# Left-over edge tiles of four edge passes: first record and gather at the start of the pass, message in three bf16 pieces, sums added bank by bank, last placing DMAs from two engines

## The reference

```python
x = _layernorm(x + gat(x))      # three attention layers
# edge layer ("edges"):
h = maximum(concat([x[row], edge_attr], 1) @ W1a + b1a, 0) @ W1b + b1b
ssum = segment_sum(h, col, N)   # then mean, an MLP, residual, norm
# relation layer ("relations"):
for r in range(8):
    out += segment_sum(where(edge_type == r, x[src] @ weight[r], 0), dst, N)
# two-layer signed GCN ("near", then "far"), for w+ and w-:
agg = segment_sum(h[src] * (dinv[src] * w * dinv[tgt])[:, None], tgt, N)
```

## Time and profile before

| | us |
|---|---|
| median of 3 runs | 4453.6 (4448.56 to 4459.53) |
| profiled execution, its span | 4502.7 |
| TensorE busy | 3132.8 (70%) |
| VectorE busy | 3224.2 (72%) |
| ScalarE busy | 1435.4 (32%) |
| GpSimd busy | 1405.7 (31%) |

### The profile page before, as it was taken

One profiled execution on the slowest core, in us unless ns is written; L12 is line 12 of the kernel. 1 busy time (PEld: TensorE's weight loads), 2 busy tenths in 40 slices (PEclk: granted clock), 3 DMA queues, 4 the chain that ended last, 5 costly groups with the idle time before them and its releaser, 6 DMA issues. The chain is left out here.

```text
span 4502.7 us, 84639 instructions
## 1 busy us (share of the span) xinstructions
PE 3132.8 (70%) x29061; PEld 2437.5 (54%) x29061; DVE 3224.2 (72%) x7791; ACT 1435.4 (32%) x2737; POOL 1405.7 (31%) x1198
## 2 busy tenths in 40 slices
PE   0087777777238348158499985588888769959995
PEld 0054444444102112112499984287888769959995
DVE  7766666665489699699577763377767579967886
ACT  0034444444025125035399981233333200000000
POOL 0055555555264454554000000266666300000000
PEclk9978888888569679579699996599999879979997
DMA  8845555545458358267377740111111024413331
GB/s 323 322 129 143 153 144 148 157 131 149 147 172 264 114 166 263 88 200 246 106 221 221 222 148 12 56 24 23 24 23 24 14 67 111 109 28 102 88 91 47
DMA packets 413507, 587.19 MB, mean 130 GB/s; under 512 B 76420, under 2 KB 301787, under 8 KB 412709
## 3 DMA queue, kind: packets, MB, share of 16 engines
q1 hardware_dynamic: 366005, 447.98, 34.2%
q0 software_dynamic: 37728, 66.91, 5.5%
q10 hardware_dynamic: 9360, 66.90, 3.7%
HBM read 340.05 MB, written 234.93 MB: 128 GB/s over the span
## 5 line engine op out<-in xcount | busy, mean ns | idle before, releaser
L846 POOL DMA_INDIRECT slots<-bc_rec,idx x496 | 484.6, 977 | 410.4 <-ACT bc_rec L807 294.4
L1284 POOL DMA_INDIRECT rp_rows<-rel_rows,slot_rel x390 | 412.1, 1057 | 431.7 <-POOLq L118 182.3
L1106 PE MATMUL psum<-a_probs,z 128*65 128x512 f32 (+1 forms) x1050 | 445.7, 557 | 145.0 <-DVE a_probs L1039 145.0
L1320 DVE TENSOR_SCALAR rp_hot_src<-rp_key_rows,lane 128x384 bf16<-128x384 f16 x1560 | 383.5, 317 | 202.0 <-issue 88.5
L1534 PE MATMUL psum<-rel_pieces,rp_hot_src 128*128 128x192 bf16 x4680 | 452.1, 249 | 94.3 <-issue 75.8
L1074 ACT ACTIVATE a_tops<-a_tops,a_s_low 128x1024 f32<-128x1024 f32 (+2 forms) x300 | 284.1, 947 | 569.6 <-DVE a_tops L1030 569.1
L1534 PEld LDWEIGHTS psum<-rel_pieces,rp_hot_src 128*128 128x128 bf16 x4680 | 390.4, 99 | 128.8 <-issue 107.0
L483 POOL DMA_INDIRECT slots<-h,idx x192 | 327.6, 1706 | 352.3 <-DMA h<-recs 304.1
L1106 PEld LDWEIGHTS psum<-a_probs,z 128*65 128x65 f32 x1050 | 121.8, 137 | 469.4 <-DVE a_probs L1039 301.5
L703 DVE TENSOR_SCALAR bc_first_t<-bc_ramp,bc_key_t 128x128 f16<-128x128 f16 x500 | 136.5, 273 | 307.8 <-PE psum L729 172.7
L1030 DVE SCALAR_TENSOR_TENSOR a_tops<-table,a_s_rest,big 128x1024 f32<-128x1024 f32 (+2 forms) x300 | 309.3, 1031 | 32.8 <-DMA big<-shift_rows 32.8
(11 more groups left out here) (438 smaller groups left out, 6855.1 us busy)
## 6 DMA issues: line engine op xcount, KB each, us to landing
a_counts<-edge_counts SPq DMA_DIRECT2D x150, 512.0 KB
slots<-big ACTq DMA_DIRECT2D x65, 1005.0 KB
ep_rec<-slots SPq DMA_DIRECT2D x65, 1005.0 KB, 6.2
edge_counts<-bc_counts SPq DMA_DIRECT2D x12, 3125.0 KB
hot_rows<-ep_hot_src SPq DMA_DIRECT2D x325, 96.0 KB, 4.5
sp_hot_src<-hot_rows SPq DMA_DIRECT2D x325, 96.0 KB, 2.0
sq_hot_src<-hot_rows SPq DMA_DIRECT2D x325, 96.0 KB, 2.0
a_counts<-edge_counts SPq DMA_DIRECT2D x75, 282.5 KB
```

The source lines that it names most:

```text
L846: pool.indirect_dma_start(k.slots, bass.IndirectOffsetOnAxis(k.idx[:, first + t:first + t + 1], 0), rec[:, j, t, :], None).then_inc(scatte ...
L1106: last = nc.tensor.matmul(sums[:, a:b], k.z[:, s, 0:D + 1], probs[:, a:b], start=s == 0, stop=True, skip_group_check=True)
L1284: pool.indirect_dma_start(rows[:, n % ROW_SLOTS, s, 0:width], None, table, bass.IndirectOffsetOnAxis(k.slot_rel[:, at:at + 1], 0))\
L1320: last = v.tensor_scalar(hot_src[:, n % HOT_SLOTS, rel, :], key_rows[:, n % 2, :], k.lane[:, rel:rel + 1], None, ALU.is_equal)
```

## The change

It touches `edge_pass`, and a little of the sorting before it.

- SP loads the first left-over tile's record as its first instruction of the pass. VectorE makes `left_no` from it before its first chunk, and POOL gathers `left_row` before its own first fetch. The loop then loads the record and gathers the rows of the tile that comes next. It does so after the last tile too, so the list gets a second tile of zero records (`zero_idx` has two columns, and one more scatter clears them).
- `left_message`: VectorE makes the one-hot matrix in bf16 instead of float32, then the message, and splits the message into three bf16 pieces with four more operations. None of it waits for the evacuation or the placing.
- TensorE does three bf16 matmuls for each of the 25 tiles (75, and in `ep` 75 more with 3 columns). It posts `left_sum` once for each bank of four tiles, and only bank 6 waits for the evacuation.
- VectorE waits for the placing DMAs behind the message and adds each bank when it is posted. Ahead of the last bank it waits for the record of the next tile and makes the next `left_no`. In `rp` the two halves of `acc` are added after the loop.
- SP issues that next record's load when all seven banks are posted. POOL, in its loop, gathers the next rows and waits until they have landed.
- The DMAs that place the last triple are issued by SP and ACT in turn, two each.

```diff
-                pool.indirect_dma_start(k.slots, bass.IndirectOffsetOnAxis(k.zero_idx[:, 0:1], 0),
+                for y in range(2):
+                    pool.indirect_dma_start(k.slots, bass.IndirectOffsetOnAxis(k.zero_idx[:, y:y + 1], 0),
...
-        left_row, left_out = sb("left_row", [P, width]), sb("left_out", [P, FIELD])
-        left_dst = k.big
+        left_row, left_out, left_rest = sb("left_row", [P, width]), sb("left_out", [P, FIELD]), sb("left_rest", [P, FIELD])
+        left_parts = sb("left_parts", [P, 3, FIELD], BF16)
+        left_dst = k.big[:, :, :].rearrange("p t c -> p (t c)").bitcast(BF16)[:, 0:NPAD].rearrange("p (t c) -> p t c", c=P)
+        left_cols = {"edges": FIELD, "relations": D}.get(kind, H)
+        LEFT_BANKS = (NT + 3) // 4
+        LEFT_STEPS = {"edges": 6, "relations": 5, "near": 6, "far": 5}[kind]
...
+        def last_parts():
+
+            j = NTRIPLE - 1
+            return [(k.acc[at:at + rows_now, tile, 0:wide], totals[m:m + rows_now, j % 2, b % SLOTS, :])
+                    for b in bins_of(j) for m, rows_now, tile, at in bin_parts(b)]
...
+                def place_last():
+                    sp.wait_ge(evacuated, NTRIPLE)
+                    for to, source in last_parts()[0::2]:
+                        sp.dma_start(to, source).then_inc(placed[(NTRIPLE - 1) % 2], 16)
...
+                sp.dma_start(left_rec[:, :], k.slots[LEFT:LEFT + P, :]).then_inc(left_in, 16)
...
-                for j in range(placed_to, NTRIPLE):
+                for j in range(placed_to, NTRIPLE - 1):
                     place(j)
+                place_last()
                 left_count = sp.value_load(k.left_tiles[0:1, 0:1], min_val=1, max_val=EPAD // P)
                 with sp.Fori(0, left_count) as i:
-                    sp.wait_ge(left_free, i + 1)
+                    sp.wait_ge(left_sum, i * LEFT_BANKS + LEFT_BANKS)
                     sp.sem_inc(fence, 1)
-                    sp.dma_start(left_rec[:, :], k.slots[bass.ds(i * P + LEFT, P), :]).then_inc(left_in, 16)
+                    sp.dma_start(left_rec[:, :], k.slots[bass.ds(i * P + LEFT + P, P), :]).then_inc(left_in, 16)
...
+                pool.wait_ge(left_idx, 1)
+                pool.indirect_dma_start(left_row[:, :], None, table,
+                                        bass.IndirectOffsetOnAxis(left_no[:, 0:1], 0)).then_inc(left_rows, 16)
...
-                    pool.wait_ge(left_idx, i + 1)
+                    pool.wait_ge(left_idx, i + 2)
                     pool.sem_inc(fence, 1)
                     pool.indirect_dma_start(left_row[:, :], None, table,
                                             bass.IndirectOffsetOnAxis(left_no[:, 0:1], 0)).then_inc(left_rows, 16)
+                    pool.wait_ge(left_rows, i * 16 + 32)
+                    pool.sem_inc(fence, 1)
...
+                def left_message(i):
+                    taken = 0
+
+                    def link(ins):
+                        nonlocal taken
+                        taken += 1
+                        ins.then_inc(left_step, 1)
+                        dve.wait_ge(left_step, i * LEFT_STEPS + taken)
+                        dve.sem_inc(fence, 1)
+
+                    out = left_out[:, 0:left_cols]
+                    v.tensor_scalar(left_dst, k.all_rows[:, :, :], left_rec[:, H + 4:H + 5], None, ALU.is_equal)\
+                        .then_inc(left_hot, 1)
+                    dve.wait_ge(left_rows, i * 16 + 16)
+                    dve.sem_inc(fence, 1)
...
+                    rest = left_rest[:, 0:left_cols]
+                    link(v.tensor_copy(left_parts[:, 0, 0:left_cols], out))
+                    link(v.tensor_tensor(rest, out, left_parts[:, 0, 0:left_cols], ALU.subtract))
+                    link(v.tensor_copy(left_parts[:, 1, 0:left_cols], rest))
+                    v.tensor_tensor(left_parts[:, 2, 0:left_cols], rest, left_parts[:, 1, 0:left_cols], ALU.subtract)\
+                        .then_inc(left_msg, 1)
...
+                dve.wait_ge(left_in, 16)
+                left_number()
...
-                dve.sem_inc(left_free, 1)
-                dve.wait_ge(evacuated, NTRIPLE)
-                for y in range(2):
-                    dve.wait_ge(placed[y], parts_placed(y, NTRIPLE))
-                if relations:
-                    chain.link(v.tensor_tensor(k.acc[:, :, 0:D], k.acc[:, :, 0:D], k.acc[:, :, D:2 * D], ALU.add))
                 left_count = dve.value_load(k.left_tiles[0:1, 0:1], min_val=1, max_val=EPAD // P)
                 with dve.Fori(0, left_count) as i:
-                    dve.wait_ge(left_in, i * 16 + 16)
+                    left_message(i)
+                    for y in range(2):
+                        dve.wait_ge(placed[y], parts_placed(y, NTRIPLE))
                     dve.sem_inc(fence, 1)
...
-                    dve.sem_inc(left_msg, 1)
-                    dve.wait_ge(left_sum, i + 1)
-                    dve.sem_inc(fence, 1)
-                    to, main = k.acc, D if relations else H
-                    for b in range(0, NT, 4):
-                        n = min(4, NT - b)
-                        bank = k.psum[:, b // 4, :].rearrange("p (t c) -> p t c", c=P)
-                        last = v.tensor_tensor(to[:, b:b + n, 0:main], to[:, b:b + n, 0:main], bank[:, 0:n, 0:main], ALU.add)
+                    for b in range(LEFT_BANKS):
+                        if b == LEFT_BANKS - 1:
+                            dve.wait_ge(left_in, i * 16 + 32)
+                            dve.sem_inc(fence, 1)
+                            left_number()
+                        dve.wait_ge(left_sum, i * LEFT_BANKS + b + 1)
+                        dve.sem_inc(fence, 1)
+                        first, n = 4 * b, min(4, NT - 4 * b)
+                        main = min(left_cols, H)
+                        bank = k.psum[:, b, :].rearrange("p (t c) -> p t c", c=P)
+                        to = k.acc[:, first:first + n, 0:main]
+                        last = v.tensor_tensor(to, to, bank[:, 0:n, 0:main], ALU.add)
                     if edges:
                         last = v.tensor_tensor(k.acc[:, :, H:FIELD], k.acc[:, :, H:FIELD],
                                                k.psum[:, 7, 0:NT * 3].rearrange("p (t c) -> p t c", c=3), ALU.add)
-                    last.then_inc(left_free, 1)
-                dve.wait_ge(left_free, 2)
+                    last.then_inc(left_step, 1)
+                    dve.wait_ge(left_step, i * LEFT_STEPS + LEFT_STEPS)
+                    dve.sem_inc(fence, 1)
+                if relations:
+                    chain.link(v.tensor_tensor(k.acc[:, :, 0:D], k.acc[:, :, 0:D], k.acc[:, :, D:2 * D], ALU.add))
...
+                act.wait_ge(evacuated, NTRIPLE)
+                for to, source in last_parts()[1::2]:
+                    act.dma_start(to, source).then_inc(placed[(NTRIPLE - 1) % 2], 16)
...
-                pe.wait_ge(evacuated, NTRIPLE)
...
-                    main = D if relations else H
-                    got = left_row if relations else left_out
+                    main = min(left_cols, H)
                     for t in range(NT):
-                        last = nc.tensor.matmul(k.psum[:, t // 4, t % 4 * P:t % 4 * P + main], left_dst[:, t, :],
-                                                left_out[:, 0:main], start=t % 4 == 0, stop=True, skip_group_check=True)
+                        if t // 4 == 6 and t % 4 == 0:
+                            pe.wait_ge(evacuated, NTRIPLE)
+                        for piece in range(3):
+                            last = nc.tensor.matmul(k.psum[:, t // 4, t % 4 * P:t % 4 * P + main], left_dst[:, t, :],
+                                                    left_parts[:, piece, 0:main], start=t % 4 == 0 and piece == 0, stop=True,
+                                                    skip_group_check=True)
+                        if t % 4 == 3:
+                            last.then_inc(left_sum, 1)
                     if edges:
                         for t in range(NT):
-                            last = nc.tensor.matmul(k.psum[:, 7, t * 3:t * 3 + 3], left_dst[:, t, :], left_out[:, H:FIELD],
-                                                    start=t == 0, stop=True, skip_group_check=True)
+                            for piece in range(3):
+                                last = nc.tensor.matmul(k.psum[:, 7, t * 3:t * 3 + 3], left_dst[:, t, :],
+                                                        left_parts[:, piece, H:FIELD], start=t == 0 and piece == 0, stop=True,
+                                                        skip_group_check=True)
                     last.then_inc(left_sum, 1)
```

63 lines of the change are left out of this document (26 added, 37 removed).

## The result

The median went from 4456.6 to 4411.5 us (four runs each); the ratio is 0.9896, 95% interval 0.9881 to 0.9911. That is 46 us less by the ratio, 40 to 53 by its interval, where 48 were forecast. The profiled execution has a span of 4401.2 us.

What follows compares the result with a forecast made beforehand. No engine bounds it; four serial pass ends hold 124.5 us. Savings of 16.0, 14.7, 11.0 and 12.4 make 54.1, less 5.5 is 48.6; median 4406, range 4389 to 4430 for 8 in 10.

Steps and rivals of the forecast that it cites:

- starts and loops: Costs outside the pass ends: 2 us for the four starts (0 to 8), 2 for new waits and counts in loops.
- VectorE's head start is worth nothing: Rival: something else holds the message, or starts give back the gain; gain under 13 us, 4441 to 4453; chance 0.07.
- Loop entry: Each pass's end: VectorE reads `left_tiles` and enters the loop, taken as 0.97 us, perhaps as little as 0.3.
- bf16 one-hot: Each pass's end: VectorE makes the one-hot matrix in bf16, taken as 1.1 us, bounds 1.0 and 1.88.
- splits: Four operations splitting the message, each waited for: 1.22 us, about 1.0 with 64 columns; bounds 0.9 and 1.4.
- The step that takes 1.5 us off for a fall in the far pass: Full clock is assumed for TensorE's 75 matmuls, less 1.5 us should the clock fall inside the far pass.
- The three-column matmuls: Edges pass: 75 further matmuls with three columns, 3.6 us at 0.048 each, taken as 4.2 for a slow clock.
- The placing: Far pass end: placing DMAs do not hold up the sums; landing 2 us later would still cost nothing.
- The new end of each pass: TensorE's end to next phase: SP, unused record, row number, gather and barrier, 7.8 us, 2.5 dearer than before.
- The dear prices: Rival: cold TensorE, slow one-hot, long gathers and dearer starts and loops leave a gain of 30.4, 4423; chance 0.2.
- The instruction streams of the relations pass: Rival: VectorE's 162 us of waits there grow as streams shift; at half more, 4486 us; chance 0.04.
- the prediction's own signs of being wrong: Late one-hot start, relations chunks changed by over 5 us, or the unused tile's gather much over 4 us.

Runs made afterwards that it cites:

- the first pair: First profiles of the kernel before and of the changed kernel: spans 4502.7 and 4401.2 us, tails together 124.5 and 74.6 us.
- e2: Changed kernel with first record, row number and gather put behind the last chunk again; ratio 1.0011 to the kernel before.
- e6: Changed kernel with the unused record and gather skipped and the last placing awaited only ahead of bank 5; 4378.65 us, 0.9827 of the kernel before.
- e1: The changed kernel again, line for line, for a second profile; 4133.6 us against 4172.3 of the kernel before, ratio 0.9899.
- the second pair: Second profiles of the kernel before and of the changed kernel, 44.0 us apart; tails together 124.7 and 80.9 us.

## Why the prediction held, and where it didn't

**Right by the sum, in part by luck.** Forecast 4406, measured 4411.5; a gain of 48 against 45.0. Forecast tails 54.1 us shorter, measured 49.9 in the first pair and 43.8 in the second. One pass missed by 9.5 us, the other three by 5.2 the other way, and 4 us taken off for starts and loops are not seen in the profiles. The mechanism held in three passes and failed in the fourth.

**The head start, right.** It was said that everything up to the message waits only for VectorE's last chunk. The one-hot matrix does start 0.2 us after it, and e2 shows that without it nothing of the gain is left. The rival "VectorE's head start is worth nothing" falls with it.

**Loop entry, bf16 one-hot, splits.** 0.97 was taken for the entry and it was 0.23, below the lower bound of 0.3: VectorE's sequencer had read `left_tiles` by then. The one-hot matrix took 1.05 (1.1). The four splits took 1.6 to TensorE's start (1.22, bound 1.4), since each starts 0.38 to 0.43 us after the one before: gaps of 0.15, not 0.04.

**TensorE.** Full clock was assumed in all four passes, and in the first profile it was granted (1.00): 4.41 us for 75 (5.15), 2.38 in relations (4.15). In the second profile relations had 0.56 and 3.90 us. The step that takes 1.5 us off for a fall in the far pass was wrong there, but such a fall did come in near in e6. The three-column matmuls took 2.02 us, not 4.2; with 0.7 at the entry that is why edges gained 19.1 and not 16.0.

**The placing, too little margin.** The first sum was to start 1.5 to 2.5 us after TensorE, and it took 2.7 in far. The prediction held that a placing landed 2 us later would still cost nothing. The margin was 0.3 us: the six sums ended at 4365.17 and the row number ran at 4365.48. In the far pass of e1 the first sum started at 4092.54, 5.25 us after the placing's first issue in place of 3.45, and the tail was 17.6 us in place of 15.9.

**The new end of each pass.** Forecast 7.8 us from TensorE's end to the next phase; 8.0 to 8.2 in edges, near and far. The row number came 2.1 to 2.3 us after TensorE's end (2.4). The gather took 0.94 or 0.95 us in all three (0.95) once nothing of VectorE's lay beside it.

**The relations pass, wrong.** The failed step reads "From TensorE's end to the next phase: 0.3 + 2.09 + 0.15 + 3.95 + 1.25", applied to all four. In relations it was 19.6 us (3499.18 to 3518.74), 11.5 more than in far. 9.0 of that is POOL's drain (9.21 in place of 0.22), which the sum did not have: the prediction took its 5.28 us of before from the far pass and did not look at what each engine does between its last instruction and the barrier. 1.0 is SP, which issues its record 1.3 us after TensorE's end in place of 0.3, because placing and the count stood before it. 1.35 is the `acc` sum beside the gather (2.29 in place of 0.94), which the sum held to cost nothing. The tail gained 5.2, not 14.7. What hid this from the result were edges, near and far, with 5.2 us more than forecast, and the starts. Nor is this a matter of one profile: in the second pair the relations tail gained 2.1.

The Trainium skill ("SBUF — State Buffer", section "SBUF: two separate sides") names VectorE operations with two SBUF inputs as holders of the shared port against a GpSimd operation that reads SBUF. The trace agrees, with 2.29 us beside L1478, which is such an operation, and 0.94 without. That the gather counts as one that reads SBUF, by its row numbers, is not shown by any run here.

**The starts, too dear.** 2 us (0 to 8) were taken for the four starts. From the first instruction of the phase ahead to a pass's first look-up, or first `rp_hot_src`, it was 159.5, 60.7 and 59.1 us before and 158.6, 59.5 and 58.9 after, in the order of the passes. Nothing was lost there. That the timed gain (46, 40 to 53 by the interval) is 3 to 4 us below the tails is inside the interval.

**The rivals.** The dear prices: the gain of 30.4 was far off, since neither clock nor gathers fell out dear. The instruction streams of the relations pass: VectorE's waits ahead of `rp_hot_src`, first profile of the changed kernel (us, times, longest) and then the second of the kernel before, to set beside the earlier trace rows:

```profile
DVE rp_hot_src L1344 <- issue: 80.8, 39, 3.0
DVE rp_hot_src L1344 <- DMA marks_now<-edge_marks: 57.3, 34, 13.0
```

```profile
DVE rp_hot_src L1320 <- ACT rp_key_rows L1447: 49.1, 65, 3.0
```

The 162 us of the kernel before are 138 here, and in its own second profile neither wait is there. They differ between executions of one program by far more than between the two programs (the chunks of the pass took 684 and 536 us before, 660 and 550 after), and no effect of the change on them can be told from that. So one of the prediction's own signs of being wrong came (chunks of the relations pass over 5 us more or less than before: 23.9 less in one pair, 14.2 more in the other), and it says nothing of the mechanism: it asked for a steadiness that two profiles of one program do not have.

## What to carry to other kernels

A loop that loads ahead for an iteration that may not come pays its full latency at the end when it runs once: put the look-ahead under a condition, or start it where something covers it. Before putting an engine last in a chain, look at what its sequencer does between its last instruction and the barrier, not only at its busy rows; a drain that was hidden turns up in full. When a pause ahead of TensorE goes, count its clock too: the same 50 float32 records took 8.63 us after 13 idle us and 5.82 after 0.7.

## What the hardware showed that I had not expected

POOL's drain after many indirect DMAs takes 6.6 to 9.2 us beyond the last of them (0.22 with two, 2.6 with 31), in the relations pass though their data has landed. It is not only in this pass: at the end of the stage with 496 edge scatters it takes 7.9 us, from 1103.1 to 1111.0. A drain placed where POOL has time left 0.14 us at the end, and the kernel was 16 us faster for it (4117.1 against 4133.6).

Matmuls with three columns, weights loaded anew each time, took 0.027 us each in bf16 (2.02 / 75, clock 1.00) and 0.12 a record in float32 (5.92 / 50, clock 0.95).

Two stages have two levels of speed, in programs that are the same there. The chunks of the relations pass take 657 to 684 us in six profiles and 534 to 550 in the other eight; what lies ahead of the first edge pass takes 2190 to 2215 and 2018 to 2036 in the same ones. The level goes with the group of runs, never with the kernel: all thirteen runs of the kernel before in one group lie at 4449 to 4464 us, all 26 in the other at 4160 to 4191. The groups ran on different chips (9 where it is noted for the first, 13 and 6 for the second). In all six profiles of the slower level VectorE's wait ahead of `rp_hot_src` that is put down to `marks_now` is there, 39 to 74 us; in none of the other eight. What sets the level stays open.
